# A graph layer with a residual and a layer norm: x in any tile slot, second loads last and summed over bands in PSUM

## The chip, the cores and the metric

One core of a Trainium2 chip runs the kernel. The metric is the device time of one execution in microseconds; the time of a kernel is the median of several runs.

## The reference

x is 8192 x 128 and adj is 8192 x 8192, both float32; w is 128 x 128.

```
A = adj + eye(8192)
deg = sum(A, axis=1)
d = rsqrt(deg)
h = (A * d[:, None] * d[None, :]) @ x
y = x + elu(h @ w)
out = layernorm(y, axis=-1, eps=1e-5)      # no scale, no shift
```

Row u of h needs every d[t], so every row sum of adj, before it is complete. adj is 256 MiB and does not fit on the chip: a part of it has to be read twice, once for its row sums and once to be multiplied.

## The kernel before

**Tiles.** adj is cut into 16 x 16 squares of 512 x 512 (1 MB each). A square (t, u) has the rows of row block u and the columns of band t. Band t of x, scaled by d[t], is its partner in the product: h[u] gets the sum over t of square (t, u) times d[t] x[t]. One square fills one of 19 tile slots (`SLOTS`), 2048 elements on each of 128 partitions.

**Loads.** There are three kinds. A *far* load reads a piece of a row block to the right of what is kept, up to 2048 columns wide, for its row sums alone, and gives its slot back after ACT has summed it. A *first* load reads a square for its row sums and its product. An *again* load reads a square for its product alone; its sums came from a far load. `kept_units()` chooses the squares (t, r) with t >= r that are loaded in row block r and stay until d[t] is known, at most `KEEP` = 12 at a time. `strip_loads(r, kept)` gives the far loads and the kept squares of a row block. The kernel's list has 329 loads: 73 far, 184 first, 72 again.

**One square's way.** SP loads it (line 488). ACT sums its rows in four activations with an accumulator (line 537). DVE turns it in place in 32 x 32 blocks (line 651); a diagonal square first gets the identity added on POOL (line 505). PE multiplies it (line 632). When a row block's sums are complete, DVE adds them up (657), POOL takes the power -0.5 (511), DVE scales the band of x (663), and DVE and ACT copy it 16 times, in quarters, into the `xs` ring of three bands (10 copies at line 670, 6 at line 545), so that each of the four 32-row quadrants of PE has every part of it. Band t may take its place in the ring when the last product of band t - 3 is done (`wait_xs_free`).

**Products.** One product takes one to four squares (`MERGE`) of one band whose slots lie at even distances: 64 matmuls with K = 32, each recorded as two, so 128 in the trace, whose moving side is 128 columns for each square. It writes one of two PSUM sets of four banks (`SETS`), one bank to a quadrant. DVE then adds the four banks to `hT` in SBUF (`add`, line 682, or 684 for a row block's first). There are 135 products.

**The end of a row block.** When all 16 squares of a row block are added, PE multiplies h by w (`out`, line 618, in a PSUM set), ACT scales it (`z`, 569), makes both relus and the exponential (576 to 579), DVE joins them (689), POOL adds the residual x (516), DVE makes mean and variance (697, 703), POOL makes rstd (522, 526), DVE normalises (709), and ACT's queue stores (586). Three tile slots (`LATE`) become the buffers of this part once all row blocks are in.

**The order.** `plan()` plays the whole run through in Python with a price for each step, gives every engine a list in the order in which things come ready there, and the engines work through their lists, waiting on semaphores. Each wait holds back all that stands behind it on that engine. `next_load()` picks loads: first loads while fewer than `FEED` = 8 squares are under way, *urgent* ones (first or again) of bands three behind the row block, else the next of the row block. The again loads so come between the row blocks from the ninth on: 41 of the 72 are issued before the last first load. `next_product()` takes the largest group at hand, a single square if there is no other.

## Time and profile before

| | us |
|---|---|
| median of 3 runs | 1122.17 (1121.51 to 1123.5) |
| the profiled execution, its own time | 1121.2 |
| its span, from first to last instruction | 1119.4 |
| DMA traffic | 359.07 MB, mean 321 GB/s |
| mean granted TensorE clock | 0.956 of full speed |

The span is what the trace shows; the execution's own time has what lies around it as well. Busy time of PE is that of its matmuls; PEld is the weight load beside it. Matmul ends are modelled. A share of the DMA engines can come out slightly over 1.

### The profile page before, as it was taken

To read this page: it belongs to the slowest core of one execution; us is meant where nothing else is said; L and a number is where in the kernel's file an instruction comes from. 1 tells how busy PE (TensorE), PEld (TensorE's weight loads), DVE (VectorE), ACT (ScalarE), POOL (GpSimd) and SP (SyncE) were. 2 spreads that over 40 slices of the span, in tenths; PEclk is the share of its full clock that TensorE was granted. 3 is DMA by queue.
4 is the path that set the end of the run, shared out by engine and by line. 5 is a ranking of instruction groups with operands and counts; after the bars stand their busy time and mean duration, and the time that the engine had idled before them with its cause. 6 is when DMAs were issued, how large, how long until landed. Compare 5 with 4: busy or idle time off the path is not lost.

```text
span 1119.4 us, 38626 instructions
## 1 busy us (share of the span) xinstructions
PE 942.1 (84%) x17408; PEld 856.9 (77%) x17408; DVE 857.2 (77%) x870; ACT 720.1 (64%) x1865; POOL 78.9 (7%) x87
## 2 busy tenths in 40 slices
PE   0089399599496798899899999999999999999992
PEld 0089388488386688889898999989889899867682
DVE  0677676765756696978899999997879987889746
ACT  6899898978977799979996857454352210133134
POOL 0000000000000000000000000000000000023124
PEclk9999789799799899999999999999999999999996
DMA  9999999989999699989999999897889868989312
GB/s 379 384 396 405 383 355 402 375 320 400 347 387 388 230 388 378 386 318 384 395 356 388 369 327 315 300 316 252 287 284 334 306 201 296 299 261 324 105 40 76
DMA packets 173764, 359.07 MB, mean 321 GB/s; under 512 B 6048, under 2 KB 30752, under 8 KB 166432
## 3 DMA queue, kind: packets, MB, share of 16 engines
q1 hardware_dynamic: 156704, 348.21, 85.9%
q10 hardware_dynamic: 16896, 8.39, 2.6%
q8 instruction: 137, 2.24, 0.8%
q14 instruction: 27, 0.22, 0.1%
HBM read 352.39 MB, written 4.19 MB: 319 GB/s over the span
## 4 chain that ended last, share of the span: by engine, by line
PE 67%; issue 10%; DMA 8%; DVE 6%; SPq 3%; ACT 3%; POOL 3%; POOLq 0%; DVEq 0%
PE p_set L632 67%; DMA tile<-in_adj 8%; SPq L488 3%; DVE tile L651 3%; ACT tile L537 2%; DVE xs L670 1%; POOL tile L516 1%; POOL rstd L526 1%; ACT xs L545 1%; DVE hT L682 1%; SPq L481 0%; POOL var_eps L522 0%; DVE tile L709 0%; DVE xn L663 0%; DVE stats L697 0%
## 5 line engine op out<-in xcount | busy, mean ns | idle before, releaser
L632 PE MATMUL p_set<-tile,xs 32*128 32x256 f32 (+3 forms) x17280 | 924.0, 371 | 154.1 <-ACT xs L545 91.9
L632 PEld LDWEIGHTS p_set<-tile,xs 32*128 32x128 f32 x17280 | 840.9, 190 | 234.3 <-issue 165.5
L537 ACT ACTIVATE tile<-tile 128x512 f32<-128x512 f32 (+2 forms) x828 | 594.3, 719 | 200.8 <-DMA tile<-in_adj 192.6
L651 DVE STREAM_TRANSPOSE tile<-tile 128x2048 f32<-128x2048 f32 x256 | 579.9, 2291 | 77.2 <-ACT tile L537 73.8
L682 DVE TENSOR_TENSOR hT<-p_set,hT 128x512 f32<-128x512 f32 (+1 forms) x202 | 151.2, 780 | 131.7 <-PE p_set L632 130.9
L537 ACT ACTIVATION_READ_ACCUMULATOR tile<-tile 128x1 f32 x828 | 154.5, 187 | 0.0
L545 ACT ACTIVATE xs<-xn 32x512 f32<-32x512 f32 x96 | 60.1, 626 | 73.5 <-PE p_set L632 55.0
L569 ACT ACTIVATE tile<-p_set,d 128x128 f32<-128x128 f32 x64 | 18.2, 366 | 104.5 <-PE p_set L618 104.5
L505 POOL TENSOR_TENSOR tile<-tile,ident 128x512 f32<-128x512 f32 x16 | 20.4, 1272 | 783.8 <-ACT tile L537 783.8
L670 DVE COPY xs<-xn 32x512 f32<-32x512 f32 x160 | 67.8, 424 | 4.2 <-PE p_set L632 1.9
L516 POOL TENSOR_TENSOR tile<-tile 128x512 f32<-128x512 f32 x16 | 20.4, 1276 | 127.6 <-DVE tile L689 127.5
L684 DVE COPY hT<-p_set 128x512 f32<-128x512 f32 (+2 forms) x10 | 10.0, 1000 | 22.4 <-PE p_set L632 22.4
L709 DVE TENSOR_SCALAR tile<-tile,mv,rstd 128x128 f32<-128x128 f32 x64 | 20.5, 383 | 4.3 <-POOL rstd L526 4.2
L511 POOL TENSOR_TENSOR d<-deg,half 128x4 f32<-128x4 f32 x16 | 16.3, 1020 | 97.0 <-DVE deg L657 96.9
L618 PEld LDWEIGHTS p_set<-w_sb,hT 128*128 128x128 f32 x128 | 16.0, 197 | 9.1 <-issue 3.6
L618 PE MATMUL p_set<-w_sb,hT 128*128 128x128 f32 x128 | 19.0, 294 | 4.4 <-DVE hT L682 2.4
L689 DVE SCALAR_TENSOR_TENSOR tile<-tile 128x512 f32<-128x512 f32 x16 | 10.9, 679 | 12.1 <-ACT tile L579 12.1
L697 DVE BATCH_NORM_STATS2 stats<-tile 128x6 f32<-128x128 f32 x64 | 13.8, 278 | 4.8 <-POOL tile L516 4.8
L526 POOL TENSOR_TENSOR rstd<-var_eps,half 128x4 f32<-128x4 f32 x16 | 16.6, 1037 | 1.3
L576 ACT ACTIVATE tile<-tile 128x512 f32<-128x512 f32 x16 | 10.1, 630 | 1.6 <-DVE tile L709 1.2
L663 DVE TENSOR_TENSOR xn<-xn,d 128x512 f32<-128x512 f32 x16 | 10.5, 657 | 0.0
L578 ACT ACTIVATE tile<-tile 128x512 f32<-128x512 f32 x16 | 10.1, 630 | 0.5
(14 smaller groups left out, 27.2 us busy)
## 6 DMA issues: line engine op xcount, KB each, us to landing
tile<-in_adj SPq DMA_DIRECT2D x325, 1024.0 KB, 11.2
xn<-in_x SPq DMA_DIRECT2D x16, 256.0 KB, 11.7
tile<-in_x ACTq DMA_DIRECT2D x16, 256.0 KB, 3.1
out_rows<-tile ACTq DMA_DIRECT2D x16, 256.0 KB, 3.4
tile<-in_adj SPq DMA_DIRECT2D x4, 768.0 KB, 10.2
w_sb<-in_w SPq DMA_DIRECT2D x1, 64.0 KB, 2.0
```

The lines of the kernel that those rows point to most:

```text
L488: sp.dma_start(shaped(k), source(loads[k])).then_inc(loaded[slot_of[k]], 16)
L505: nc.gpsimd.tensor_tensor(on_diagonal, on_diagonal, ident[:, :].unsqueeze(1).to_broadcast([128, BLOCKS, 128]), ALU.add)\
L516: nc.gpsimd.tensor_tensor(pos[:, n % RING], pos[:, n % RING], res[:, n % RING], ALU.add).then_inc(y_ready, 1)
L526: nc.gpsimd.tensor_tensor(rstd[:, n % RING], var_eps[:, :], half[:, :], ALU.pow).then_inc(rstd_ready, 1)
L537: ins = nc.scalar.activation(view[:, g], view[:, g], ACT.Copy, accum_out=to[:, g:g + 1])
L545: ins = nc.scalar.activation(xs_part(t, q, s), xn[quadrant(s), t % XN], ACT.Copy)
L618: ins = nc.tensor.matmul(p[:, 0, F * b:F * (b + 1)], hT[:, at:at + 128], w_sb[:, :], start=True, stop=True)
L632: ins = nc.tensor.matmul(to, xs[quadrant(q), t % XRING, j], turned[quadrant(q), j], start=j == 0, stop=j == GROUPS - 1)
L651: nc.vector.transpose(tiles[slot_of[k]], tiles[slot_of[k]]).then_inc(tile_turned, 1)
L670: ins = nc.vector.tensor_copy(xs_part(t, q, s), xn[quadrant(s), t % XN])
L682: nc.vector.tensor_tensor(rows, new, rows, ALU.add).then_inc(product_added, 1)
L709: ins = nc.vector.tensor_scalar(pos[:, n % RING, b], pos[:, n % RING, b], mv[:, n % RING, b, 0:1], rstd[:, n % RING, b:b + 1], ALU.subtrac ...
```

## The change

- Slots: 22 tile slots and no `xs` ring. A band of scaled x takes any free slot (a *home*) when its row block's loads are issued, and gives it back when the band's first squares are multiplied; bands 13 and up, and all that are at home once the rows are in, keep it until their again squares are done too.
- All again loads come after the last row block, by groups of two row blocks (three in the first where their number is odd) from the last rows to the first. Bands whose x has left are loaded, scaled and copied anew (`recopy`, all 16 copies on ACT).
- A group's squares of all bands are summed in one PSUM set by several *parts*; one add follows. A part takes a band's squares of both row blocks, if their slots allow, else one. First squares still make a product (a job with one part) each; a single one is taken only when no other square of its band is coming.
- `KEEP` is 12 below row block 9 and 10 from there on; `FEED` is 10; a row block's loads wait while a band more than two behind has first squares left (`AHEAD`).
- PE waits for the copies of x by steps (those of one s), not for all 16.
- ACT normalises (Identity with scale and bias), after DVE has made shift = -mean * rstd.
- An out takes whichever PSUM set is free.

```diff
@@ -10,25 +10,27 @@
 BANDS = N // BAND
 BLOCKS = BAND // 128
 GROUPS = BAND // 32
-SLOTS = 19
+SLOTS = 22
 LATE = 3
-KEEP = 12
-XRING = 3
+KEEP = (12, 9, 10)
+AHEAD = 2
+STAY = 13
 XN = 2
-COPIES = {"dve": [(s, q) for s in (0, 1) for q in range(Q)] + [(2, 0), (2, 1)], "act": [(2, 2), (2, 3)] + [(3, q) for q in range(Q)]}
 RING = 4
 SETS = 2
 MERGE = 4
-FEED = 8
+FEED = 10
 FLIGHT = 4
 EPS = 1e-5
+COPIES = {"dve": [(s, q) for s in (0, 1) for q in range(Q)] + [(2, 0), (2, 1)], "act": [(2, 2), (2, 3)] + [(3, q) for q in range(Q)]}
+ALL_COPIES = [(s, q) for s in range(Q) for q in range(Q)]
 
 
 def kept_units():
 
     alive, kept = [0] * BANDS, set()
     for t, r in sorted(((t, r) for t in range(BANDS) for r in range(t + 1)), key=lambda v: (v[0], -v[1])):
-        if all(alive[m] < KEEP for m in range(r, t + 1)):
...
+def row_groups(agains):
+
+    rows = sorted({u for _, _, u in agains}, reverse=True)
+    sizes = [3] + [2] * len(rows) if len(rows) % 2 else [2] * len(rows)
+    groups = []
+    while rows:
+        n = sizes.pop(0)
+        groups.append([v for v in agains if v[2] in rows[:n]])
+        rows = rows[n:]
+    return groups
...
+    def take_slot(tenant):
+        freed, slot = min(free)
+        free.remove((freed, slot))
+        tenants[slot].append(tenant)
+        return slot
+
+    def ask_x(t):
+
+        nonlocal dma
+        if not free or len(homes) >= XN and copied.get(len(homes) - XN) != 2:
+            return False
+        home_of[t] = len(homes)
+        homes.append((t, take_slot(("home", len(homes)))))
+        order["sp"].append(("x", home_of[t]))
+        dma = max(dma, now + 1.0) + XLOAD
+        if t in known:
+            offer("dve", 5, "scale", home_of[t], 0.7)
+        return True
+
+    def drop_home(t):
+        release(homes[home_of.pop(t)][1])
...
-        last = at_row - XRING
-        urgent = [v for v in firsts + agains if v[1] <= last]
-        pending = sorted(firsts + agains, key=lambda v: (v[2], v[1])) if rows_done and len(x_asked) == BANDS else []
-        pick = pending[0] if pending else urgent[0] if urgent else firsts[0] if firsts else agains[0] if agains and rows_done else None
-        if pick and backlog < FEED:
-            (firsts if pick[0] == "first" else agains).remove(pick)
-            return pick
-        if row_todo and not (row_todo[0][0] == "first" and len(slots) < 2):
+        oldest = min((t for t in range(BANDS) if first_left[t]), default=BANDS)
+        if row_todo and at_row > oldest + AHEAD:
+            pick_row = False
+        else:
+            pick_row = bool(row_todo) and not (row_todo[0][0] == "first" and len(free) < 2)
+        if firsts and (backlog < FEED or not pick_row):
+            return firsts.pop(0)
+        if pick_row:
             return row_todo.pop(0)
-        if pick and len(slots) > 1:
-            (firsts if pick[0] == "first" else agains).remove(pick)
-            return pick
+        if rows_done and not firsts and not row_todo:
+            return next_again()
         return None
+
+    def next_again():
+
+        nonlocal group_at, group_todo
+        if len(late) < LATE:
+            return None
+        if not group_todo:
+            if group_at + 1 == len(last_groups):
+                return None
+            bands = sorted({v[1] for v in last_groups[group_at + 1]}, reverse=True)
+            for t in bands:
+                if t not in home_of and not ask_x(t):
+                    return None
+            group_at += 1
+            group_todo = sorted(last_groups[group_at], key=lambda v: (v[1] if group_at == 0 else -v[1], v[2]))
+            group_open.append([set(last_groups[group_at]), sorted({v[2] for v in last_groups[group_at]})])
+            if not free:
+                return None
+        return group_todo.pop(0)
...
+            known.add(arg)
+            offer("dve", 0, "scale", home_of[arg], 0.7)
         elif kind == "scale":
-            offer("dve", 0, "copies", arg, 0.4 * len(COPIES["dve"]))
-            offer("act", 0, "copies", arg, 0.62 * len(COPIES["act"]))
-        elif kind == "copies":
-            copied[arg] = copied.get(arg, 0) + 1
+            if sum(1 for h, (t, _) in enumerate(homes) if t == homes[arg][0] and h < arg):
+                offer("act", 4, "recopy", arg, 0.64 * len(ALL_COPIES))
+            else:
+                offer("dve", 0, "copies", arg, 0.43 * len(COPIES["dve"]))
+                offer("act", 0, "copies", arg, 0.64 * len(COPIES["act"]))
+        elif kind in ("copies", "recopy"):
+            copied[arg] = copied.get(arg, 0) + (1 if kind == "copies" else 2)
...
+            if not first_left[t] and (not again_left[t] or t < STAY and not rows_done):
+                drop_home(t)
+            if last:
+                offer("dve", 1, "add", job, 0.15 + 0.55 * len(jobs[job][1]))
...
-            offer("dve", 2, "normalise", arg, 1.5)
+            offer("dve", 2, "shift", arg, 0.2)
+        elif kind == "shift":
+            offer("act", 1, "normalise", arg, 1.5)
...
+    def next_part():
+
+        nonlocal group_job
+        if free_set() is not None:
+            groups = [even_slots([k for k in tiles_ready if loads[k][0] == "first" and loads[k][1] == t]) for t in range(BANDS)]
+            groups = [g for g in groups if len(g) > 1 or g and not any(loads[k][:2] == ("first", loads[g[0]][1]) for k in coming)]
+            if groups:
+                ks = max(groups, key=lambda g: (min(len(g), 2), -loads[g[0]][1]))
+                for k in ks:
+                    tiles_ready.remove(k)
+                job = open_job([loads[k][2] for k in ks], {loads[k][2]: 1 for k in ks})
+                parts.append((job, home_of[loads[ks[0]][1]], ks, True, True))
+                return len(parts) - 1
+        if group_open and (group_job is not None or free_set() is not None):
+            left, rows = group_open[0]
+            here = [k for k in tiles_ready if loads[k] in left]
+            for t in sorted({loads[k][1] for k in here}, reverse=True):
+                ks = sorted((k for k in here if loads[k][1] == t), key=lambda k: loads[k][2])
+                want = [v for v in left if v[1] == t]
+                if len(ks) < len(want):
+                    continue
+                at = [slot_of[k] for k in ks]
+                gaps = {b - a for a, b in zip(at, at[1:])}
+                if len(gaps) > 1 or any(abs(g) > 15 for g in gaps):
+                    ks = ks[:1]
+                first = group_job is None
+                if first:
+                    group_job = open_job(rows, {u: sum(v[2] == u for v in left) for u in rows})
+                for k in ks:
+                    tiles_ready.remove(k)
+                    left.remove(loads[k])
+                parts.append((group_job, home_of[t], ks, first, not left))
+                if not left:
+                    group_job = None
+                    group_open.pop(0)
+                return len(parts) - 1
+        return None
+
+    out_set = {}
...
+            def normalise(n):
+
+                act.wait_ge(shift_ready, n + 1)
+                for b in range(BLOCKS):
+                    ins = nc.scalar.activation(pos[:, n % RING, b], pos[:, n % RING, b], ACT.Identity,
+                                               bias=shift[:, n % RING, b:b + 1], scale=rstd[:, n % RING, b:b + 1])
+                ins.then_inc(normed, 1)
...
+                job, h, ks, first, last = parts[arg]
+                bank, rows, _ = jobs[job]
+                if first:
+                    wait_set_free(pe, ("job", job))
+                pe.wait_ge(tile_turned, max(turn_nth[k] for k in ks))
+                at = [slot_of[k] for k in ks]
+                column = 128 * rows.index(loads[ks[0]][2])
+                assert [loads[k][2] for k in ks] == rows[column // 128:column // 128 + len(ks)]
+                for s in range(Q):
+                    if h in recopied:
+                        pe.wait_ge(copied_by["act"], copied["act"][h] + Q * (s + 1))
+                    else:
+                        for engine in ("dve", "act"):
+                            some = [i for i, c in enumerate(COPIES[engine]) if c[0] == s]
+                            if some:
+                                pe.wait_ge(copied_by[engine], copied[engine][h] + max(some) + 1)
+                    for b in range(BLOCKS):
+                        j = Q * b + s
                         for q in range(Q):
-                            to = p[:, q, 0:128 * len(at)]
-                            to = to.rearrange("f (g i) -> f g i" if len(at) == 1 else "f (n g i) -> f n g i", g=BLOCKS, i=32)
-                            ins = nc.tensor.matmul(to, xs[quadrant(q), t % XRING, j], turned[quadrant(q), j],
-                                                   start=j == 0, stop=j == GROUPS - 1)
-                    ins.then_inc(product_out, 1)
+                            chunk = tile[quadrant(q), at[0], 32 * j:32 * j + 32]
+                            step = at[1] - at[0] if len(at) > 1 else 1
+                            moving = bass.AP(chunk.tensor, chunk.offset, [[SLOTS * 2048, 32], [2048 * step, len(at)], [BAND, BLOCKS], [1, 32]])
+                            to = p_set[bank][:, q, column:column + 128 * len(at)].rearrange("f (n g i) -> f n g i", g=BLOCKS, i=32)
+                            ins = nc.tensor.matmul(to, xs_of(h)[quadrant(q), j], moving, start=first and s == b == 0, stop=last and s == b == 3)
+                ins.then_inc(part_out, 1)
...
-                    for b in range(BLOCKS):
-                        ins = nc.vector.tensor_scalar(pos[:, n % RING, b], pos[:, n % RING, b], mv[:, n % RING, b, 0:1],
-                                                      rstd[:, n % RING, b:b + 1], ALU.subtract, ALU.mult)
-                    ins.then_inc(normed, 1)
+                    if n >= RING:
+                        dve.wait_ge(normed, n - RING + 1)
+                    nc.vector.scalar_tensor_tensor(out=shift[:, n % RING], in0=mv[:, n % RING, :, 0], scalar=-1.0, in1=rstd[:, n % RING],
+                                                   op0=ALU.mult, op1=ALU.mult).then_inc(shift_ready, 1)
 
 
 # ---- launch: one core; inputs and output as the reference has them ----
```

## Rows read from the trace of the kernel before

**Rows 1.** page, busy us, share and instructions of each engine

```profile
PE 942.1 (84%) x17408; PEld 856.9 (77%) x17408; DVE 857.2 (77%) x870; ACT 720.1 (64%) x1865; POOL 78.9 (7%) x87
```

**Rows 2.** windows: from:to, length, engines' busy us, clock, DMA share, GB/s

```profile
56.00:560.00 504.00, 416.19 (x8297) 382.85 (x8301) 363.95 (x288) 438.23 (x1116) 15.93 (x14) 0.93 0.99 369
...
560.00:1094.00 534.00, 521.36 (x9087) 470.13 (x9080) 457.62 (x500) 226.55 (x630) 47.68 (x50) 1.00 0.83 281
...
56.00:112.00 56.00, 50.86 (x1088) 50.27 (x1092) 41.54 (x24) 52.12 (x128) 0.00 (x0) 0.97 1.04 400
...
448.00:504.00 56.00, 50.42 (x1188) 48.10 (x1184) 45.83 (x39) 47.00 (x127) 2.29 (x2) 0.97 0.97 352
...
504.00:560.00 56.00, 53.14 (x1104) 49.59 (x1100) 48.97 (x38) 52.14 (x143) 2.25 (x2) 1.00 1.05 390
...
560.00:616.00 56.00, 55.98 (x1019) 50.89 (x1015) 52.66 (x46) 43.20 (x121) 2.29 (x2) 1.00 1.02 372
```

**Rows 3.** waits of SP's queue, 0:560, then 560:1120; total, times, longest

```profile
SPq L488 <- PE p_set L632: 201.5, 51, 16.9
...
SPq L488 <- ACT tile L537: 97.6, 43, 15.7
...
SPq L488 <- PE p_set L632: 375.8, 63, 18.3
...
SPq L488 <- ACT tile L537: 6.8, 3, 4.0
```

**Rows 4.** waits of PE, 560 to 1120 us, first and last of four

```profile
PE p_set L632 <- DVE hT L682: 5.6, 8, 1.6
...
PE p_set L618 <- ACT tile L569: 2.1, 2, 1.7
```

**Rows 5.** a full stretch of PE; in the timeline two singles and a pair

```profile
L632 PE MATMUL p_set<-tile,xs 32*128 32x256 f32 (+2 forms) x2048 | 104.2, 361 | 1.6 <-DVE hT L682 1.6
...
356.15 3.85 PE L632 MATMUL p_set<-tile,xs 32*128 32x128 f32 x127 [2.17 <-issue]
...
1072.50 7.19 PE L632 MATMUL p_set<-tile,xs 32*128 32x256 f32 x128 [0.32 <-DVE hT L682]
...
1089.70 3.85 PE L632 MATMUL p_set<-tile,xs 32*128 32x128 f32 x128 [0.32 <-DVE hT L682]
```

**Rows 6.** groups by form, whole run: busy us, mean ns, idle before

```profile
L651 DVE STREAM_TRANSPOSE tile<-tile 128x2048 f32<-128x2048 f32 x256 | 579.9, 2291 | 77.2 <-ACT tile L537 73.8 <-POOL tile L505 2.7
...
L682 DVE TENSOR_TENSOR hT<-p_set,hT 128x512 f32<-128x512 f32 x166 | 107.0, 680 | 91.4 <-PE p_set L632 90.8
...
L545 ACT ACTIVATE xs<-xn 32x512 f32<-32x512 f32 x96 | 60.1, 626 | 73.5 <-PE p_set L632 55.0 <-DVE xn L663 17.5
...
L709 DVE TENSOR_SCALAR tile<-tile,mv,rstd 128x128 f32<-128x128 f32 x64 | 20.5, 383 | 4.3 <-POOL rstd L526 4.2
...
L569 ACT ACTIVATE tile<-p_set,d 128x128 f32<-128x128 f32 x64 | 18.2, 366 | 104.5 <-PE p_set L618 104.5
...
L663 DVE TENSOR_TENSOR xn<-xn,d 128x512 f32<-128x512 f32 x16 | 10.5, 657 | 0.0
```

**Rows 7.** timeline of the end: out, its rstd, the last product's out

```profile
1079.62 1.16 PE L618 MATMUL p_set<-w_sb,hT 128*128 128x128 f32 x8
...
1087.67 1.04 POOL L526 TENSOR_TENSOR rstd<-var_eps,half 128x4 f32<-128x4 f32 x1
...
1093.48 2.05 PE L618 MATMUL p_set<-w_sb,hT 128*128 128x128 f32 x16
```

**Rows 8.** loads: landings and issues of SP; issues by kind, median landing

```profile
DMA to landing us min/median/max: 4.8/11.1/27.1
...
L488 SPq DMA_DIRECT2D tile<-in_adj x200: 327/724/9181, 1.2 to 568.4; - x100
...
xn<-in_x SPq DMA_DIRECT2D x16, 256.0 KB, 11.7
...
out_rows<-tile ACTq DMA_DIRECT2D x16, 256.0 KB, 3.4
```

More of the change, by code:

```diff
@@ L88, in sum_took, with free_set, allowed @@
         return 0.1 + BLOCKS * (BAND / 1200 + 0.2)
-    def allowed(engine, kind, arg):
-        if engine == "pe" and len(turns) >= SETS and len(turns) - SETS not in released:
-            return False
+    def free_set():
+        return next((s for s in range(SETS) if set_user[s] is None), None)
+    def allowed(kind, arg):
         if kind == "out":
-            return len(late) == LATE and counts["outs"] == counts["z"]
+            return free_set() is not None and len(late) == LATE and counts["outs"] == counts["z"]
         if kind == "z":
             return counts["stored"] >= arg - RING + 1
-        if kind == "scale":
-            return arg in x_asked
-        if kind == "copies":
-            return arg < XRING or not tiles_left[arg - XRING]
         return True
@@ L105, in release @@
         if rows_done and len(late) < LATE:
+            tenants[slot].append(("late", len(late)))
             late.append(slot)
@@ L307, in plan @@
             finished(*arg)
-    assert sum(len(ks) for _, ks in products) == BANDS * BANDS, sum(len(ks) for _, ks in products)
+    assert sum(len(p[2]) for p in parts) == BANDS * BANDS, sum(len(p[2]) for p in parts)
     assert len(finals) == BANDS and counts["stored"] == BANDS
-    return loads, slot_of, late, products, finals, order, turns, (now, busy, dma)
+    return loads, slot_of, homes, tenants, late, jobs, parts, finals, order, turns, (now, busy, dma)
 def gcn_resnorm(nc: bass.Bass, x: bass.AP, adj: bass.AP, w: bass.AP, out: bass.AP):
@@ L317, in gcn_resnorm @@
     AX = mybir.AxisListType
-    loads, slot_of, late, products, finals, order, turns, _ = plan()
+    loads, slot_of, homes, tenants, late, jobs, parts, finals, order, turns, _ = plan()
     def nth_of(engine, kind):
         return {arg: n + 1 for n, arg in enumerate(a for k, a in order[engine] if k == kind)}
-    sum_nth, turn_nth = nth_of("act", "sum"), nth_of("dve", "turn")
+    sum_nth, turn_nth, diagonal_nth = nth_of("act", "sum"), nth_of("dve", "turn"), nth_of("pool", "diagonal")
+    row_nth, power_nth = nth_of("dve", "row_sum"), nth_of("pool", "power")
+    scale_nth, z_nth = nth_of("dve", "scale"), nth_of("act", "z")
+    part_of = {k: i for i, p in enumerate(parts) for k in p[2]}
+    last_part = {h: max(i for i, p in enumerate(parts) if p[1] == h) for h in range(len(homes))}
+    job_end = {p[0]: i for i, p in enumerate(parts) if p[4]}
+    copied = {"dve": {}, "act": {}}
+    for engine in ("dve", "act"):
+        done = 0
+        for kind, h in order[engine]:
+            if kind in ("copies", "recopy"):
+                copied[engine][h] = done
+                done += len(COPIES[engine]) if kind == "copies" else len(ALL_COPIES)
+    recopied = {h for kind, h in order["act"] if kind == "recopy"}
+    arrived, counts = [], [0] * SLOTS
+    for k in range(len(loads)):
+        counts[slot_of[k]] += 16
+        arrived.append(counts[slot_of[k]])
+    before = {tenant: row[i - 1] if i else None for row in tenants for i, tenant in enumerate(row)}
+    summed_rows = {r: [] for r in range(BANDS)}
+    for k, load in enumerate(loads):
+        if load[0] != "again":
+            summed_rows[load[1] if load[0] == "far" else load[2]].append(k)
     adds, begun = [], {}
-    for n in (a[0] for k, a in order["dve"] if k == "add"):
-        for i, k in enumerate(products[n][1]):
-            u = loads[k][2]
-            last = adds[-1] if adds and adds[-1][0] == n else None
+    for job in (a for k, a in order["dve"] if k == "add"):
+        for i, u in enumerate(jobs[job][1]):
+            last = adds[-1] if adds and adds[-1][0] == job else None
             if last and u == last[2] + last[3] and bool(last[4]) == (u in begun):
```

307 lines of the change are left out of this document (147 added, 160 removed).

## The prediction

> **What bounds the kernel now.** I read the page's busy shares first, and they mislead: PE, DVE and ACT at 84, 77 and 64% [rows 1] look like a kernel with room everywhere. The windows by stage say otherwise [rows 2]. There are three stages with different limits.
>
> From 56 to 560 us the DMA engines sit at a share of 0.99 (the fullest window shows 1.04 at 400 GB/s), and PE works 416 of 504 us. Here the loads set the pace, and PE's gaps cost nothing unless they hold slots back. From 560 to 1094 us PE works 521 of 534 us with DMA at 0.83: PE sets the pace. The waits of SP's queue agree [rows 3]: after 560 us it waits 375.8 us for products to free slots and 6.8 us for sums. PE itself then waits for almost nothing: 14.7 us over the four entries of its waits, 8.0 of them for adds on DVE [rows 4]. After 1094 us comes the epilogue of the last rows: the last product ends at 1093.5 us and the span at 1119.4, 25.9 us later [rows 7].
>
> **What a tile costs PE.** Counted along the kernel's own list, the 16 products of 643.4 to 747.7 us are 30 tiles, three of them alone in their product: 104.2 us, 3.47 us a tile [rows 5]. A single late in the run takes 3.85 us and a pair 7.19, 3.60 a tile. An early single shows 3.85 us behind 2.2 us of "issue" [rows 5]. So a single costs PE 0.3 to 0.4 us more than half a pair where PE is the bound, and some 2.6 more only where the DMA sets the pace anyway. The list has 135 products: 35 singles, 80 pairs, 19 triples, one quadruple. At 560 us the matmul count (8,334 in the windows, 128 to a product) puts PE at product 65, with 114 of 256 tiles done; 142 tiles remain.
>
> **The change, part by part.**
>
> *Number of loads.* Following kept_units() with KEEP 12 and 10 gives 61 kept tiles where there were 64, hence 75 second loads for 72, and 75 far loads for 73. Second loads come in the PE-bound stage and still every tile is multiplied once: 256 tiles either way, so PE's work is the same. Rows 0 to 8 need 207 loads (far, kept and the others) in both kernels. The DMA-bound stage is therefore as long as before by this count. 0 us.
>
> *Slots.* 19 tile slots and 3 fixed x buffers become 22 slots, of which each living band of x takes one. In the row stage two or three bands live, so zero or one slot is won; from row 9 on two more, because KEEP falls to 10. If this kept DMA at the 400 GB/s of its fullest window instead of 369 over the 504 us, it would save 504 x (1 - 369/400) = 39 us; if it wins nothing, 0. SP's waits in that stage, 201.5 us for PE and 97.6 us for ACT, mostly pass while earlier transfers are still in flight, since the share is 0.99. A share of 1.04 would give 24 us. I take a fifth of that, -5 us. A loss is possible too, since singles are now held back for a partner and free their slots later: up to one turn and one landing, say +8 us in all, an estimate from the 2.3 and 11.2 us of [rows 6, 8].
>
> *Copies released step by step.* PE may start after 4 of 16 copies: at most 3 us earlier (six ACT copies of 0.63 us [rows 6] shrink to the first step's), once, ahead of the first product; later bands have it inside the DMA-bound stage. It lies inside the range of the -5.
>
> *Fewer products.* In 560 to 1094 us the list has 11 singles; the second loads now go in pairs wherever a row pair shares a band. Two-row groups are {11,10}, {9,8}, {7,6}, {5,4}, {3,2}, {1,0} with 2, 9, 10, 14, 20 and 20 tiles, and only 3 tiles have no partner. -4 us: 11 x 0.38. More waits stand inside a product (4 to 8), but a pair spends 28 ns an instruction where a single gets through in 15 (7.19 and 3.85 us over 256), so they have room. 0 us; with 0.06 us each on 40 products, about 15 us as the worst case.
>
> *Sums in PSUM, outs spread.* 72 second tiles lose their adds on DVE (0.68 us each, at most 49 us [rows 6]), replaced by six of 1.2 us. DVE is 86% busy after 560 us [rows 2], and PE waits for it only 8 us [rows 4]; together with ACT-bound turns at the outs and issue that is 14.7 us, of which I take 7 as won, since outs now come two at a time between long groups instead of one after another. -7 us.
>
> *Normalise moved to ACT.* 20.5 us leave DVE and about 64 x 0.37 = 24 us land on ACT [rows 6], which works 227 of 534 us there. Hidden; 0 us but for the last row, +0.5 us.
>
> *The tail.* Before, five outs crowd in after 1088 us and the chain ends 25.9 us after the last product [rows 7]. One row alone takes, from its out at 1079.62 to rstd's end at 1088.71, 9.1 us; then 1.1 for normalise, 0.5 and 3.4 for the store: 14.1 us. The last group ends two rows at once: add 1.5 us, the row's 14.1, and 3.1 for the second row behind the first's z and relus (1.14 + 1.9), plus 0.5 and gaps: 20 us. -6 us.
>
> *Rows without second loads between them.* Before, second loads fill PE from product 71 (about 590 us). Now nothing does until all rows are in. With first loads alone PE worked 103.6 of 112 us just before 560, and 56.0 of 56 just after. The remaining rows bring fewer loads than PE time: 200 loads are issued by 568.4 us [rows 8], which leaves 56 of the 256 (75 far, 61 kept, 120 other first ones) at 2.7 us (1.05 MB at 390 GB/s), 151 us, against 181 - 114 = 67 tiles, 232 us. So PE should stay nearly full; +4 us, between 0 and 19 (below).
>
> *Bands copied anew.* Bands 6 to 12 have given up their slots when their second loads come: 7 more x loads, 7 scales (0.66 us), and 7 x 16 ACT copies of 0.63 us, 70 us on an ACT that has the time. On PE's path they matter only where loads are held: the third band of group {5,4} is asked for after the first is copied, 11.7 us to land, 0.7 to scale, 10.1 to copy [rows 6, 8]: 23 us, and then 11.2 + 2.3 for the first tile, 36 us. 14 slots of waiting tiles (22 less 3 of the epilogue and 5 of x) are 49 us of PE. Hidden if they are full. The wait for three epilogue slots at the start of the second loads is about 10 us against 16 ready tiles. +2.5 us, between 0 and 30.
>
> Sum: -5 - 4 - 7 - 6 + 0.5 + 4 + 2.5 = -15 us. The profiled span of 1119.4 becomes 1104.4; that execution took 1121.2 us, 1.8 more than its span, and the median of the runs is 1.0 above it. So 1107 us, 1.3% faster. A change of 0.2%, 2 us, is about what this kernel's measurement can tell.
>
> **Rivals.**
>
> *A, the early stage wakes up.* The slots do what they might, and the DMA share goes to 1.04: 24 us for my 5, 1088 us, and 1073 at 400 GB/s. For it: SP waits nearly 300 us there. Against: the engines are at 0.99 while it waits.
>
> *B, rows starve PE.* Bands 12 to 15 have only 6, 6, 6 and 4 first tiles, 14 to 21 us of PE, while from the last load to copied x takes about 25 us. If the 67 tiles after 560 us run at the 92.5% that 448 to 560 us shows, the stage costs 19 us in place of 4: 1122 us, no change. The Trainium skill (Perfetto Trace Analysis, Optimization Strategy) advises interleaving regimes in which different engines are the most contended, and this change separates them. By that rule B is the case to expect; the trace is with it only up to 560 us.
>
> *C, too few slots at the end, slower.* The last two groups need ten bands of x; with three epilogue slots nine are left for tiles. A slot's round is 11.2 us to land, 4.6 for two turns, 7.2 in the product, 0.5 to issue: 23.5 us, and nine slots then give a tile every 2.6 us, faster than PE's 3.47. It decides once the round passes 31 us, a landing of 19; the longest seen is 27.1 [rows 8]. If those 40 tiles came every 4.2 us, +29 us, 1136 us. Stalls for the copied bands would come at the same place.
>
> *D, nothing that counts changes*, the PE-bound work being the same: -15 us turns into about 0 because the waits at the outs come back elsewhere and the tail keeps its length: 1121 us.
>
> **How the numbers follow.** Forecast 0.45 (its own range 1095 to 1115); A 0.15; B 0.13; C 0.20; D 0.07. Faster are the forecast, A and a part of B: 0.67. Slower are C and a few of B and D: 0.24. Same: 0.09. The range takes A's middle and C's better half: 1080 to 1132.
>
> **What would show it.** Right: DMA share near 1.0 until about 590 us and PE as full after it as before; no second load before about 800 us; about 120 parts and six long sums; outs in pairs, the last two within 2 us of the last part; 20 us from the last part to the end. Wrong: PE gaps behind x copies or turns between 650 and 850 us (B); PE waiting for turns, those for landings, in the last 140 us (C); a DMA share over 1.02 early (A). I should be wrong most easily in the first stage, where a slot more or less shifts when every row becomes known.

## The result, and the profile after

The changed kernel takes 1089.87 us (median of 4 runs, 1089.42 to 1092.27) beside 1122.69 us before (now 4 runs): a ratio of 0.9713, 95% interval 0.9696 to 0.973. That is 2.9% faster where I had forecast 1.3%. The direction was right, and the gain is more than twice as large as forecast. The time lies inside the range of 1080 to 1132 us, close to the 1088 us of rival A. The profiled span is 1087.7 us, 31.7 less than before.

Windows of the changed kernel by the same three stages (columns as in [rows 2]). The last part ends at 1068.2 us.

```profile
56.00:560.00 504.00, 432.10 (x7044) 362.38 (x7048) 393.02 (x313) 465.30 (x1198) 18.05 (x16) 0.93 1.04 392
560.00:1068.00 508.00, 494.70 (x9072) 466.89 (x9068) 388.72 (x410) 291.42 (x723) 52.31 (x56) 0.99 0.84 284
1068.00:1088.00 20.00, 2.50 (x20) 1.94 (x16) 6.38 (x21) 9.02 (x22) 5.37 (x6) 0.65 0.09 26
```

The first line is the news. DMA has gone from 369 to 392 GB/s, share 0.99 to 1.04, over 504 us. Counted along the kernel's list, 7,044 matmuls are 55.0 parts and 120.1 tiles; before, 8,297 were 64.8 products and 111.6 tiles. (The prediction said 114: I had taken the tile count behind product number 65 instead of behind 65 products.) So some 8.5 more tiles are multiplied at 560 us (8.4 before the counts are rounded), 31 us of PE at the 3.7 us a tile, outs and gaps included, that both kernels need afterwards. They come in larger groups: the first 55 parts hold 5 single squares, the first 64 products before held 25.

SP's queue up to 560 us, waits in total, times, longest; to be set beside [rows 3]:

```profile
SPq L611 <- PE p_set L772: 105.5, 35, 9.2
SPq L611 <- ACT tile L660: 99.3, 55, 5.8
```

The waits for products have halved, from 201.5 us, and the longest has shrunk from 16.9 to 9.2. One window shows what such a wait does. This is 336 to 392 us, first in the kernel before:

```profile
336.00:392.00 56.00, 38.78 (x872) 36.12 (x869) 35.20 (x33) 42.12 (x106) 2.30 (x2) 0.88 0.84 309
...
SPq L488 <- PE p_set L632: 34.7, 6, 16.9
```

and then in the changed one:

```profile
336.00:392.00 56.00, 50.00 (x708) 35.45 (x704) 44.67 (x37) 52.16 (x137) 2.29 (x2) 0.94 1.04 394
```

Before, SP waited 34.7 us there for PE, once 16.9 us on end, and the transfers ran dry; now it waits 7.5 us for PE and as long for ACT. PE does more work with fewer matmuls (708 for 872): it works on groups of three and four squares there, where before it took one single after another until 365 us.

What PE waits for in the whole changed run, the three largest of six entries ([rows 4] has only the part after 560 us):

```profile
PE p_set L772 <- DVE tile L790: 59.5, 1, 59.5
PE p_set L772 <- DVE tile L810: 57.6, 5, 18.7
PE p_set L772 <- DVE hT L821: 15.9, 6, 7.2
```

The first two are the start and the changes of band while DMA sets the pace. Nothing waits for x copies (L810) after 560 us; rival B's gap is not there.

The timeline of the end, where before the last product ended at 1093.5 us [rows 7]:

```profile
1068.28 1.22 DVE L821 TENSOR_TENSOR hT<-p_set,hT 128x1024 f32<-128x1024 f32 x1 [26.24 <-PE p_set L772]
1069.65 1.13 PE L746 MATMUL p_set<-w_sb,hT 128*128 128x128 f32 x8 [1.44 <-DVE hT L821]
1072.01 1.16 PE L746 MATMUL p_set<-w_sb,hT 128*128 128x128 f32 x8 [1.23 <-ACT tile L686]
...
1084.94 0.38 ACTq L711 DMA_DIRECT2D out_rows<-tile  x1
```

One add for the pair of row blocks (DVE idle for 26 us before it, its turns all done), two outs, two rows behind each other, the last store issued at 1084.94. From the last part to the end: 19.5 us, before 25.9.

Together: between 560 us and the last part or product, 135.9 tiles took 508.2 us, 3.74 each; before, 144.4 took 533.5, 3.695 each. That is 5.8 us lost. At 3.695 us a tile the 8.4 tiles are 31.1 us won before 560 us, and 6.4 are won in the tail: 31.1 + 6.4 - 5.8 = 31.7 us. (How the sum splits into 31.1 and 5.8 hangs on the price of a tile.) The loss has a place, 784 to 896 us, the groups of row blocks down to {5,4}:

```profile
784.00:896.00 112.00, 101.94 (x1884) 93.87 (x1884) 77.02 (x115) 67.73 (x138) 21.53 (x26) 0.95 0.78 247
```

PE works 101.9 of 112 us where it worked 109.2 in the same window before.

### The profile page after: what moved, and what is told of

It is laid out like the page before. It is cut to its first block, busy times and chain, and to the rows that moved or that the text cites. A ratio compares the mean times of both kernels' runs of the same rounds, so it can differ in the third digit from the quotient of the medians.

```text
span 1087.7 us, 36085 instructions
## 1 busy us (share of the span) xinstructions
PE 929.3 (85%) x16128; PEld 831.2 (76%) x16128; DVE 807.2 (74%) x761; ACT 809.3 (74%) x2033; POOL 78.7 (7%) x87
## 4 chain that ended last, share of the span: by engine, by line
PE 38%; issue 24%; DMA 21%; ACT 5%; DVE 4%; SPq 4%; POOL 3%; POOLq 0%; DVEq 0%
PE p_set L772 38%; DMA tile<-in_adj 20%; ACT tile L660 4%; SPq L611 4%; DVE tile L810 2%; POOL tile L639 1%; POOL rstd L649 1%; DVE hT L821 1%; DMA xn<-in_x 1%; DVE tile L790 1%; POOL tile L628 1%; DVE xn L803 0%; POOL var_eps L645 0%; ACT tile L668 0%; PE p_set L746 0%
## 5 line engine op out<-in xcount | busy, mean ns | idle before, releaser
L772 PE MATMUL p_set<-tile 32*128 32x256 f32 (+3 forms) x16000 | 912.5, 386 | 138.6 <-DVE tile L790 59.5
L772 PEld LDWEIGHTS p_set<-tile 32*128 32x128 f32 x16000 | 815.7, 189 | 231.2 <-issue 141.9
L668 ACT ACTIVATE tile<-xn 32x512 f32<-32x512 f32 x208 | 130.4, 627 | 31.6 <-DVE xn L803 24.1
L821 DVE TENSOR_TENSOR hT<-p_set,hT 128x512 f32<-128x512 f32 (+1 forms) x137 | 109.0, 828 | 55.2 <-PE p_set L772 54.5
L810 DVE COPY tile<-xn 32x512 f32<-32x512 f32 x160 | 66.8, 418 | 5.0
L702 ACT ACTIVATE tile<-tile,shift,rstd 128x128 f32<-128x128 f32 x64 | 26.1, 485 | 29.1 <-DVE shift L849 29.1
L803 DVE TENSOR_TENSOR xn<-xn,d 128x512 f32<-128x512 f32 x23 | 15.2, 660 | 11.8 <-DMA xn<-in_x 11.8
L823 DVE COPY hT<-p_set 128x1024 f32<-128x1024 f32 (+1 forms) x7 | 9.6, 1372 | 18.7 <-PE p_set L772 18.7
L649 POOL TENSOR_TENSOR rstd<-var_eps,half 128x4 f32<-128x4 f32 x16 | 16.6, 1037 | 1.3
L695 ACT ACTIVATE tile<-tile 128x512 f32<-128x512 f32 x16 | 10.1, 630 | 0.5
L693 ACT ACTIVATE tile<-tile 128x512 f32<-128x512 f32 x16 | 10.1, 630 | 0.4
```

The source lines that it names most:

```text
L649: nc.gpsimd.tensor_tensor(rstd[:, n % RING], var_eps[:, :], half[:, :], ALU.pow).then_inc(rstd_ready, 1)
L668: nc.scalar.activation(xs_part(h, q, s), xn[quadrant(s), h % XN], ACT.Copy).then_inc(copied_by["act"], 1)
L702: ins = nc.scalar.activation(pos[:, n % RING, b], pos[:, n % RING, b], ACT.Identity, bias=shift[:, n % RING, b:b + 1], scale=rstd[:, n % R ...
L772: ins = nc.tensor.matmul(to, xs_of(h)[quadrant(q), j], moving, start=first and s == b == 0, stop=last and s == b == 3)
L810: nc.vector.tensor_copy(xs_part(h, q, s), xn[quadrant(s), h % XN]).then_inc(copied_by["dve"], 1)
L821: nc.vector.tensor_tensor(rows, new, rows, ALU.add).then_inc(product_added, 1)
```

## The experiments

Two theories stood at first: S, the three slots of the old ring are what keeps the loads going; and O, it is the generated order as a whole, in which slots are one input of several. The numbers of the changed kernel are 1089.9 us, share 1.04 and 120.1 tiles at 560 us. Times are medians; differences to the changed kernel are taken from the ratios to the kernel before, since not all ran on the same chip. Tiles are counted from the matmuls up to 560 us along each kernel's own list. Some of the texts written ahead of the runs use an earlier count, 122 tiles and 114 before, where the table has 120.1 and 111.6.

Undoing a part makes `plan()` play everything through again. Only three x buffers, all copies at once and the steps in the kernel before keep the order of loads and of PE; every other run changes the order as well, and its loss is that of both.

| | us | ratio to before (95%) | share, 56 to 560 us | tiles at 560 us |
|---|---|---|---|---|
| before | 1122.7 | 1 | 0.99 | 111.6 |
| changed | 1089.9 | 0.9713 (0.9696 to 0.973) | 1.04 | 120.1 |
| 19 slots, FEED 7 | 1111.5 | 0.9893 (0.9864 to 0.9921) | 1.01 | 114.7 |
| FEED 8 | 1134.2 | 1.0137 (1.0071 to 1.0204) | 1.03 | 117.5 |
| ring, FEED 7 | 1121.0 | 0.9982 (0.9957 to 1.0006) | 1.02 | 116.0 |
| ring alone | 1137.0 | 1.0129 (1.0073 to 1.0185) | 1.00 | 115.0 |
| singles at once | 1093.0 | 0.9769 (0.9701 to 0.9837) | 1.04 | 120.0 |
| row order | 1119.1 | 0.9969 (0.9942 to 0.9996) | 1.04 | 120.0 |
| an add for each part | 1108.2 | 0.9872 (0.9854 to 0.989) | 1.04 | 120.0 |
| all copies at once | 1098.8 | 0.9797 (0.9775 to 0.982) | 1.03 | 118.7 |
| three x buffers | 1090.5 | 0.9719 (0.9685 to 0.9753) | 1.04 | 120.0 |
| normalise on DVE | 1097.5 | 0.9773 (0.9751 to 0.9795) | 1.04 | 120.0 |
| before, steps | 1112.2 | 0.9912 (0.988 to 0.9943) | 1.00 | 113.5 |
| before, hold | 1128.2 | 1.0054 (1.0026 to 1.0082) | 1.00 | 114.9 |

**19 slots, FEED 7.**

```diff
-SLOTS = 22
+SLOTS = 19
-FEED = 10
+FEED = 7
```

> The changed kernel won about 25 of its 32 us before 560 us: DMA share 1.04 there where it was 0.99, 122 tiles multiplied at 560 us where it was 114. This kernel is the changed one with 19 tile slots in place of 22 (homes of x still among them) and FEED 7 in place of 10. Theory S (slots): the three slots of the old ring, now free for tiles, keep SP's queue from being held; with 19 slots and homes inside them there are two or three fewer tile slots than even the kernel before had, so the early share falls to 0.97 or less, and the time goes to 1130 us or more. Theory O (order): what counts is whether the generated order happens to keep loads going across the changes of band, and the number of slots is only one input to it; then with a FEED that suits 19 slots the early share stays at 1.02 or above and the time is 1095 to 1112 us.

1111.5 us with a share of 1.01. S's price of 1130 us or more is refuted; O's time came, but not its share. With three slots fewer than the changed kernel and FEED 7, 5.4 of the 8.5 tiles are gone. This run changes two things, so the share of the slots in it is not shown; the run with the ring alone, below, is the cleaner one.

**FEED 8.**

```diff
-FEED = 10
+FEED = 8
```

> The changed kernel with FEED 8 in place of 10, all 22 slots. Theory S: slots are unchanged, so the early DMA share stays near 1.04 and the time within 10 us of 1090. Theory O: the order is a different one and the early share can fall to that of the kernel before or under it (0.96 to 1.00); time 1105 to 1140 us.

Each theory is half right: 48 us separate this kernel from the changed one. The early stage stays nearly as good (1.03, 117.5 tiles), as S had it. The time is worse than before the change, as O had it, and most of what is lost comes after 560 us; the largest single piece is the change of band at 711 us. The rows of this kernel, one window and PE's timeline around the gap:

```profile
672.00:728.00 56.00, 43.81 (x836) 40.44 (x832) 33.25 (x32) 29.16 (x85) 2.29 (x2) 0.88 0.86 281
```

```profile
624.72 86.73 PE L772 MATMUL p_set<-tile 32*128 32x384 f32 x1536 [1.61 <-issue]
723.64 22.91 PE L772 MATMUL p_set<-tile 32*128 32x256 f32 x384 [12.19 <-DVE tile L810]
```

PE stands still for 12.2 us for x copies in the stage where it should set the pace. This is rival B's mechanism, caught in a neighbour of the changed kernel: no second squares are there to fill the gap.

**The ring, with FEED 7 and alone.** Bands of x may only use slots 19 to 21 until all row blocks are in; everything else takes the other 19.

```diff
...
     def take_slot(tenant):
-        freed, slot = min(free)
-        free.remove((freed, slot))
+        pool = ring if tenant[0] == "home" and not rows_done else free
+        freed, slot = min(pool)
+        pool.remove((freed, slot))
...
-        if not free or len(homes) >= XN and copied.get(len(homes) - XN) != 2:
+        if not (free if rows_done else ring) or len(homes) >= XN and copied.get(len(homes) - XN) != 2:
...
```

> The changed kernel with x bands confined to three fixed slots while rows are still being loaded, as the old ring did, 19 slots for tiles; FEED 7. It undoes the first part of the change alone. Theory S: the whole early gain is gone, share 0.99, about 114 tiles at 560 us, time 1090 + 25 = 1115 us. Theory O: time anywhere between 1100 and 1130 us, and the loss would show as a few long holds of the load queue at band changes, not as an evenly lower share.

> The changed kernel with x bands confined to three fixed slots in the row stage and nothing else changed (FEED stays 10). With FEED 7 this lost 4 of the 8.5 tiles won at 560 us and 31 us in all. Theory S, slots: tiles at 560 us fall to 112 to 116 and DMA share to 1.00 or less. With 19 tile slots and ten squares under way, 12 kept and the loads in flight, the load queue should be held at every band change, so I expect it at or above 1121 us, and up to 1160.

With FEED 7: 1121.0 us, 116.0 tiles and a share of 1.02. S had asked for the whole early gain to go (its 114 tiles are 111.6 by the count of the table) and a share of 0.99; about half of the gain went. The time fits O's range, and nearly S's 1115 us, so this run doesn't decide. Alone it is the plain undoing of the first part, and what S had asked for came: 1137.0 us, 115.0 tiles, share 1.00. Its windows, the whole stage and the one of 336 to 392 us:

```profile
56.00:560.00 504.00, 415.19 (x6228) 338.55 (x6232) 376.28 (x285) 446.06 (x1153) 15.68 (x14) 0.92 1.00 372
336.00:392.00 56.00, 44.50 (x627) 34.44 (x624) 38.42 (x30) 46.64 (x119) 2.24 (x2) 0.88 0.93 343
```

and what SP waited for from 336 to 392 us:

```profile
SPq L619 <- ACT tile L668: 22.8, 5, 16.6
SPq L619 <- PE p_set L780: 4.1, 2, 3.3
```

A long hold is back, 16.6 us on end, this time put down to ACT's sums and not to products, and the share in this window is 0.93. So giving x three slots of its own takes 5.1 of the 8.5 tiles, 19 us, with the order that goes with it. That leaves 3.4 tiles over the kernel before. The other 28 of the 47 us that this kernel loses come after 560 us: PE works 467.0 of the 500 us up to 1060, where the changed kernel works 486.7.

**Singles at once.**

```diff
-            groups = [g for g in groups if len(g) > 1 or g and not any(loads[k][:2] == ("first", loads[g[0]][1]) for k in coming)]
+            groups = [g for g in groups if g]
```

> The changed kernel, but PE takes a single square at once when it has no pair, as before, instead of holding it for a partner that is on its way. Theory H (holding for pairs): the singles of the DMA-bound stage take PE 6 us each, with issue waits, and hold slots; undoing the hold brings them back, loses 8 or more tiles by 560 us and gives 1110 us or more. Theory O or S: only the order shifts; 1090 to 1105 us.

1093.0 us, the interval reaching down to the changed kernel's ratio, and 120.0 tiles. H's 1110 us did not come. But the singles did not come back either: up to 560 us this kernel's list has 5 of them, as many as the changed one, where the kernel before has 25. So the line that holds singles back is not what keeps them few early on, and this run doesn't say what few singles are worth; the last run below does in part.

**Row order.** First squares are loaded by row block and then band, as before.

```diff
-        firsts.sort(key=lambda v: (v[1], v[2]))
+        firsts.sort(key=lambda v: (v[2], v[1]))
```

> The changed kernel with the first squares loaded in order of row block and then band, as before, instead of band by band. Band by band finishes the oldest band sooner, so its home comes free sooner and the row gate opens sooner. If that is what the early stage lives on, DMA share falls to 1.00 and tiles at 560 us to 114 or fewer, and the time rises by 20 us or more. If not, the early stage stays at 1.03 to 1.04 and what is lost comes after 560 us, as with FEED 8.

The early stage is untouched (1.04, 120.0 tiles), and it had to be: the first 226 loads of the two lists are the same, and some 209 are issued by 560 us. So the new order has no part in the early gain, and yet 29 us are lost without it, all later. Of this kernel, the window from 560 us:

```profile
560.00:784.00 224.00, 210.73 (x3822) 187.25 (x3826) 200.03 (x190) 164.43 (x469) 15.92 (x14) 0.97 0.88 304
```

PE works 210.7 of 224 us; the changed kernel works 222.6 there.

**An add for each part.** Every part of the last groups opens its own product, as before. The loads keep their order; their slots shift a little at the end, and there are 126 parts instead of 125.

```diff
-                first = group_job is None
-                if first:
-                    group_job = open_job(rows, {u: sum(v[2] == u for v in left) for u in rows})
+                if free_set() is None:
+                    return None
+                group_job = open_job([loads[k][2] for k in ks], {loads[k][2]: 1 for k in ks})
...
-                parts.append((group_job, home_of[t], ks, first, not left))
+                parts.append((group_job, home_of[t], ks, True, True))
+                group_job = None
                 if not left:
-                    group_job = None
                     group_open.pop(0)
```

> The changed kernel with its last groups' order of loads, but every part of a group is its own product with its own add on DVE, as before (some 40 adds in place of 6). My prediction gave sums in PSUM and spread outs together 7 us. If DVE is not near its limit in the last 300 us (31 to 40 us busy of 56 in the windows after 784 us), the adds hide: within 3 us of 1090. If the PSUM sums are what makes the end fast, 1097 us or more.

1108.2 us: 18 us lost, nothing early. The adds do not hide. PE's waits in this kernel, whole run:

```profile
PE p_set L772 <- DVE hT L821: 31.7, 17, 6.9
```

That is 17 waits for adds where the changed kernel has 6, and 31.7 us where it has 15.9: nearly all of the loss. DVE works 214.8 of the 300 us from 784 us, 72%, so its mean load was not the bound. Its turns take 2.3 us each, and with two PSUM sets PE waits as soon as an add stands behind one or two of them; that the turns are what the adds stand behind was not counted. The text ahead of the run had 1097 us or more for this case.

**All copies at once.** The order is the same; PE waits for all 16 copies of a band ahead of its first matmul.

```diff
-                        pe.wait_ge(copied_by["act"], copied["act"][h] + Q * (s + 1))
+                        pe.wait_ge(copied_by["act"], copied["act"][h] + len(ALL_COPIES))
...
-                            some = [i for i, c in enumerate(COPIES[engine]) if c[0] == s]
-                            if some:
-                                pe.wait_ge(copied_by[engine], copied[engine][h] + max(some) + 1)
+                            pe.wait_ge(copied_by[engine], copied[engine][h] + len(COPIES[engine]))
```

> The changed kernel in the same order, but PE waits for all copies of a band of x before its first matmul instead of step by step. My prediction: at most 3 us, at the first product. If early release at each band change matters to the slots (8 bands in the DMA-bound stage, 2 to 3 us each), the DMA share before 560 us falls from 1.04 and the time rises by 5 to 15 us.

1098.8 us: 9 us, three times the most that I had allowed. SP's waits for PE in the early stage rise from 105.5 us:

```profile
SPq L611 <- PE p_set L770: 153.7, 42, 11.8
```

At each change of band the first product, and with it the first slots, come later. While DMA sets the pace that is 1.4 tiles by 560 us, 5 us; the rest is lost later.

**The same part put into the kernel before.** Its lists are untouched; each copy signals by itself, and the matmuls of a product are put in the order of s, as in the changed kernel, so that the steps can be waited for one by one.

```diff
...
-                    for copies in ("dve", "act"):
-                        pe.wait_ge(copied_by[copies], copied[copies][t])
...
-                    for j in range(GROUPS):
+                    for n, j in enumerate(Q * g + s for s in range(Q) for g in range(BLOCKS)):
+                        if n % BLOCKS == 0:
+                            for copies in ("dve", "act"):
+                                some = [i for i, c in enumerate(COPIES[copies]) if c[0] == n // BLOCKS]
+                                if some:
+                                    pe.wait_ge(copied_by[copies], len(COPIES[copies]) * (copied[copies][t] - 1) + max(some) + 1)
...
```

> The kernel before, same lists, with one part of the change alone: every copy of x signals by itself and PE waits for the copies of one step at a time. In the changed kernel, taking this part away cost 9 us (1098.8 against 1089.9) and 1.4 tiles at 560 us. If the part has its worth by itself, because PE frees slots earlier at each of eight band changes while the DMA sets the pace, the kernel before gains 5 to 10 us: 1112 to 1117. If its worth lies only in the changed order, less than 2 us.

1112.2 us, 0.9912: 10 us and 1.9 tiles by itself. This is the one part tried in both kernels whose worth comes out the same, within the intervals, and with the order of loads and of PE kept in both.

**Three x buffers.**

```diff
-XN = 2
+XN = 3
```

> The changed kernel with three staging buffers for x (XN 3) instead of two. In the trace SP is held 19.2 us at the third band of the group of row blocks 5 and 4 until an earlier band is copied, and PE works only 50 and 52 of 56 us in the two windows from 784. If that hold is what empties PE there, 3 to 8 us are won: 1083 to 1087. If those gaps come from outs and adds in turn, nothing: 1088 to 1091.

1090.5 us, nothing won. What SP's x loads (L606) waited for from 560 us on in this kernel, where the changed one has 34.7 us in two such entries:

```profile
SPq L606 <- ACT tile L668: 0.3, 1, 0.3
```

The hold at the third band has gone and the time has not moved; the interval leaves room for 2.6 us won at most. In the changed kernel the hold did run the transfers dry (a share of 0.06 from 812 to 826 us), but PE's waits in those 14 us are for adds, not for tiles. So copying bands anew does not stall PE through the load queue by anything that shows; the half of rival C that I had priced at 36 us of latency against 49 of ready tiles is out.

**Normalise on DVE.**

```diff
-            offer("dve", 2, "shift", arg, 0.2)
-        elif kind == "shift":
-            offer("act", 1, "normalise", arg, 1.5)
+            offer("dve", 2, "normalise", arg, 1.5)
...
```

> The changed kernel with normalise back on DVE (64 x 0.38 us) instead of ACT. My prediction: hidden, and half a microsecond won back in the tail; the order of the lists moves a little. 1086 to 1095 us; more than 1095 would mean that DVE's place in the order matters at the end.

1097.5 us, 7 us slower, where I had called the move hidden. The lists shift a little with it (15 single parts instead of 11), and how much of the 7 us is the move itself this run can't tell.

**Hold in the kernel before.** A single waits for a partner of its band that is on its way.

```diff
...
+        near = [loads[k][1] for k in coming if loads[k][0] == "first"]
+        groups = [g for g in groups if len(g) > 1 or g and loads[g[0]][1] not in near]
...
```

> The kernel before with another part alone: a single square waits for a partner when one of its band is on its way. In the changed kernel, taking it away cost 3 us with an interval that includes nothing. Theory H: fewer singles in the DMA-bound stage keep slots moving; 1110 us or less. Otherwise the list shifts by itself and the result is within 10 us of 1122 on either side.

1128.2 us: 3.3 tiles more at 560 us and yet 0.5% slower. Theory H's 1110 us is refuted, but the early half of what it says came: 4 singles up to 560 us instead of 25, SP's waits for products 161.1 us instead of 201.5. And a tile won early is no time won if the order behind it fits less well.

## Why the prediction was right or wrong

**The step that failed is the one on slots**: "I take a fifth of that, -5 us". The early stage gave 8.5 tiles, 31 us. I had both ends, 39 and 24 us, and argued myself down with one sentence: that SP's waits pass while earlier transfers are still in flight, since the share is 0.99. A full queue shows 1.04 and 1.05 here, so 0.99 is a mean of full windows and dry ones, and a single window of 56 us at 0.84 was there to be read. Rival A, at 0.15, was the case, and the share over 1.02 that I had named as its sign came. That its 1088 us is so near is in part luck: A asked for 24 us in the early stage and got 31, and had the stage after 560 us 4.5 us cheaper, where it came out 5.8 us dearer. What the runs put in place of the term: 5.1 tiles (19 us) for slots that x no longer owns, undone alone but with the order replanned; 1.4 tiles for the copies released by steps, in the same order; some 2 tiles that no run here assigns, if the parts add up at all. They need not: FEED 8 has 2.6 tiles fewer than FEED 10 with free slots, while with the ring FEED 7 has 1.0 more. The strongest candidate for the 2 tiles is that singles have become few: holding them back gave the kernel before 3.3 tiles. No run here brings them back into the changed kernel. The order of first squares has no part in it.

**Copies by steps.** I allowed 3 us, once, and counted on the DMA-bound stage to hide the rest. It cost 9 us to take away and gave 10 us to the kernel before (there with the matmuls in a new order too). A DMA-bound stage hides PE's time only as long as PE's lateness doesn't hold slots; I had written this myself in the first paragraph and not applied it.

**Number of loads.** Right: 331 loads, 256 tiles, 7 bands copied anew, and no second square loaded ahead of the last first one. The second squares begin earlier than I had said, between 700 and 720 us and not at about 800.

**Sums in PSUM.** -7 us together with the outs; undoing the sums alone costs 18 us. Right in sign and too small. I had judged by DVE's busy share and the 8 us of waits for adds before; what matters, as I read the 17 waits, is how long an add may stand behind a turn when only two PSUM sets exist.

**Fewer products.** -4 us for the singles from 560 us on. The list before has 10 of them there (the prediction said 11), the changed one 6, and 11 in the whole run instead of 35. Five of those are among the second squares, where I expected three, since the slots of one pair (band 13, row blocks 4 and 5) do not lie close enough. No run isolates the term.

**Normalise.** Hidden, I said; with the shift of order that comes with it, 7 us are in it.

**The tail.** Predicted 20 us, measured 19.5, by the same chain: add, out, two rows behind each other. The two outs begin 1.4 and 3.8 us behind the last part, where I had said within 2.

**Rows without second squares, and bands copied anew.** I gave them +4 and +2.5 us. The stage from 560 us on came out 5.8 us dearer than before at equal tiles, although the terms for products and sums (-4 and -7) should have made it 11 us cheaper. So if those two held, the other two cost about 17 us in place of 6.5; if the sums were worth the 18 us that undoing them costs, about 28. Neither was measured by itself: this is the second place where the sum failed, and which of its terms did is open. The Trainium skill's advice to interleave regimes (Perfetto Trace Analysis, Optimization Strategy) bears on this: the changed kernel separates them and this stage is the one that got dearer, which agrees, while the kernel as a whole got faster; no run here puts second squares back between the rows of the changed kernel. In the changed kernel itself PE shows no gap behind x copies after 560 us; in the one with FEED 8 it shows one of 12.2 us. The sign of rival B was right for this stage, and was outweighed by the early one.

**Still open**: which part of the order makes 784 to 896 us 7 us poorer in PE work. It is not the hold of the x loads. PE's waits there are 10.1 us, and most are for adds and not for tiles: 2.6 us ahead of an out, and ahead of parts

```profile
PE p_set L772 <- DVE hT L821: 4.8, 2, 3.2
```

The longest, at 824.1 us, is for an add that DVE began at 822.8, behind a `shift` that had waited 1.2 us for POOL. In this window DVE's list also stands 18.6 us for squares to land and 11.8 us for x to land, where before it waited 10.8 us, for PE alone. That is a lead, and no run here follows it up. The last groups, where I had feared the nine slots, keep PE full: PE works 56.0 of 56 us from 952 to 1008 and again to 1064:

```profile
952.00:1008.00 56.00, 56.00 (x1028) 52.83 (x1024) 37.33 (x19) 4.57 (x11) 0.00 (x0) 1.00 0.97 319
1008.00:1064.00 56.00, 56.00 (x1028) 52.82 (x1027) 29.64 (x32) 6.11 (x15) 5.07 (x6) 1.00 0.56 201
```

Rival C is refuted in both halves, the second as far as the load queue goes. No version tried here beats the changed kernel.

## What to carry to other kernels

Find out what a full transfer queue shows in this profile before calling a stage DMA-bound: 0.99 against 1.04 over 504 us was worth 31 us, and one dry window with the longest single wait of the load queue was there to give it away. In such a stage, freeing a buffer sooner can be worth time even on an engine with slack: signalling copies one by one was worth 9 to 10 us in either kernel. Where a program orders the work by a greedy play-through, undo one part, look in the new lists whether the undoing took place in the stage in question (in singles at once and row order it had not), and read the stages apart: small constants moved this kernel by up to 48 us, and a change of order can give the same early lead and lose it all later.

## What the runs showed that I had not expected

The sum over bands in PSUM paid 18 us on an engine that was 72% busy without it. And in the stage that DMA bounds, the nine windows of 56 us from 56 to 560 us reached 400 GB/s and a share of 1.05 at most in the kernel before and went down to 309 GB/s, while the changed kernel held 383 to 400 GB/s in each of them. ACT works 465.3 of these 504 us in the changed kernel, 92% (438.2 before), so the row sums may be what binds next; nothing here tests it.
